# Neighbour maps turned by transposing transfers, the inverse deviation by logarithm and exponential, and a new order on every engine

## What is computed

```python
def L0(x):                       # a routed low-rank update
    w = softmax(x @ router_W.T + router_b)             # 8 experts
    y = einsum('bsr,nhr->bsnh', (x @ lora_A.T summed over 4), lora_B)   # lora_A is the context
    return nan_to_num(x + 0.5 * einsum('bsn,bsnh->bsh', w, y))
def L1(x):                       # cross attention on the context, 32 heads of 16, masked
    x = x + softmax(Q @ K.T / 4, masked) @ V @ Wo.T + bo
    mu = mean(x); var = mean((x - mu)**2)
    return (x - mu) / sqrt(var + 1e-5) * ln_g + ln_b
def L2(xyz, points, w_center, w_neighbor):   # run twice (L2, L3), the same weights
    d2 = squared distances between the 512 columns of xyz (the context)
    idx = top_k(-d2, 8)                       # 8 nearest columns of each
    for i in range(4):
        p = leaky_relu(points)
        c  = w_center[i] @ p
        gn = w_neighbor[i] @ gather(p, idx)   # for each of the 8 neighbours
        points = (c + gn.sum(over the 8)) / 9 + points
```

## Time and profile before

| what | value |
|---|---|
| median of 3 runs | 374.36 us (373.85 to 374.52) |
| the profiled execution's own time | 374.17 us |
| its span, first to last instruction | 372.4 us |
| PE busy | 365.6 us, 98% |
| PEld busy | 309.1 us, 83% |
| DVE busy | 217.8 us, 58% |
| ACT busy | 205.0 us, 55% |
| POOL busy | 123.8 us, 33% |
| DMA queues, share of 16 engines | 21.8% |

### The profile page before, as it was taken

How to read it: one execution, slowest core, us unless ns; L and a number is a source line. 1 busy time by engine, 2 the same in 40 slices (tenths; PEclk the granted TensorE clock), 3 DMA queues, 4 the chain that set the end, 5 groups by cost and what they waited for, 6 DMA issues and landing times.

```text
span 372.4 us, 6622 instructions
## 1 busy us (share of the span) xinstructions
PE 365.6 (98%) x2396; PEld 309.1 (83%) x2396; DVE 217.8 (58%) x363; ACT 205.0 (55%) x368; POOL 123.8 (33%) x125
## 2 busy tenths in 40 slices
PE   7999999999999999999999999999999999999996
PEld 4576898969878869787879899988988988989985
DVE  3946889897898867535667263343344434344334
ACT  2185357867569885475573665442843728166221
POOL 5068011430200724041072533441561445234500
PEclk9999999999999999999999999999999999999999
DMA  6993038107248117000000000000000000000004
GB/s 196 314 383 126 3 100 203 31 2 183 67 122 176 37 34 179 9 2 1 2 1 2 0 2 0 2 0 1 2 0 2 0 2 1 2 0 3 28 30 169
DMA packets 25057, 22.48 MB, mean 60 GB/s; under 512 B 9537, under 2 KB 20546, under 8 KB 25026
## 3 DMA queue, kind: packets, MB, share of 16 engines
q1 hardware_dynamic: 24352, 22.04, 21.1%
q10 hardware_dynamic: 674, 0.02, 0.1%
HBM read 12.35 MB, written 3.15 MB: 42 GB/s over the span
## 4 chain that ended last, share of the span: by engine, by line
PE 93%; SPq 3%; DMA 2%; issue 1%; DVE 0%; ACT 0%
PE slot L563 90%; SPq L495 2%; DMA xyz_n<-in_ctx 1%; DMA q_stack<-shiftT 1%; PE slot L683 1%; PE slot L724 1%; PE slot L692 1%; SPq L524 1%; PE slot L668 0%; DVE points L1333 0%; SPq L546 0%; PE slot L741 0%; SPq L447 0%; ACT low L881 0%; SPq L397 0%
## 5 line engine op out<-in xcount | busy, mean ns | idle before, releaser
L1080 POOL TENSOR_TENSOR p_lo<-p_full,p_hi 128x512 fp32r<-128x512 f32 x64 | 82.7, 1309 | 165.7 <-ACT p_full L1031 99.1
L1333 DVE SCALAR_TENSOR_TENSOR points<-slot,points 128x512 f32<-128x512 f32 x64 | 43.3, 689 | 65.6 <-PE slot L563 65.6
L1041 ACT ACTIVATE u_hi<-slot 128x512 fp32r<-128x512 f32 x64 | 36.9, 597 | 78.8 <-PE slot L563 78.7
L1328 DVE TENSOR_TENSOR u_lo<-slot,u_hi 128x512 fp32r<-128x512 f32 x64 | 42.9, 687 | 41.8 <-ACT u_hi L1041 41.7
L563 PE MATMUL slot<-adj,u_hi 128*128 128x512 f32 x256 | 66.0, 393 | 0.0
L563 PE MATMUL slot<-adj,u_lo 128*128 128x512 f32 x256 | 65.8, 391 | 0.0
L563 PE MATMUL slot<-fs_lo,p_hi 128*128 128x256 f32 x256 | 64.0, 283 | 0.0
L563 PE MATMUL slot<-fs_hi,p_hi 128*128 128x256 f32 x256 | 63.9, 283 | 0.0
L563 PEld LDWEIGHTS slot<-adj,u_lo 128*128 128x128 f32 x256 | 46.8, 188 | 9.1 <-DVE u_lo L1328 0.2
L563 PEld LDWEIGHTS slot<-adj,u_hi 128*128 128x128 f32 x256 | 46.0, 188 | 8.5
L563 PEld LDWEIGHTS slot<-fs_lo,p_hi 128*128 128x128 f32 x256 | 48.9, 191 | 0.6
(11 more groups left out here) (144 smaller groups left out, 552.4 us busy)
## 6 DMA issues: line engine op xcount, KB each, us to landing
q_stack<-q_hi SPq DMA_DIRECT2D x32, 128.0 KB, 2.4
x_in<-in_xT SPq DMA_DIRECT2D x8, 256.0 KB, 5.3
q_stack<-q_lo SPq DMA_DIRECT2D x16, 128.0 KB, 3.2
out_points<-points SPq DMA_DIRECT2D x8, 256.0 KB, 2.0
loraB_raw<-in_lora_BT SPq DMA_DIRECT2D x1, 1024.0 KB, 7.8
wk<-in_WkT SPq DMA_DIRECT2D x1, 1024.0 KB, 10.8
wq_raw<-in_WqT SPq DMA_DIRECT2D x1, 1024.0 KB, 10.5
wv<-in_WvT SPq DMA_DIRECT2D x1, 1024.0 KB, 11.4
```

The source lines that it names most:

```text
L1041: act.activation(half_of(u_hi[:, u], i % 2), bank("wa", b, i // 2, i % 2), ACT.Copy)\
L1080: pool.tensor_tensor(lo[:, cut], full[:, cut], hi[:, cut].bitcast(F32), ALU.subtract)\
L1328: dve.tensor_tensor(half_of(u_lo[:, u], i % 2), bank("wa", b, i // 2, i % 2), half_of(u_hi[:, u], i % 2).bitcast(F32), ALU.subtract).then_ ...
L1333: dve.scalar_tensor_tensor(pts, bank("ga", b, i // 2, i % 2), 1.0 / (TOPK + 1), pts, ALU.mult, ALU.add).then_inc(points_ready, 1)
```

## The change

1. The step `adjT` goes, on TensorE, with its two banks and the identity `ident_h` that POOL made for it. In its place SP issues, for each `near` step, one transposing transfer (`nt`) of a 128x512 piece of 2-byte values from SBUF to SBUF: 16 transfers of 128 KB. `adjC` now reads SBUF. The turned maps lie where other things lie at other times: that of entry 0 in `points[:, 0]`, of entry 1 in `points[:, 2]`, those of entries 2 and 3 in `near_late`, over the memory of the attention's stacks. So new waits come with it: `nt` of entry 1 waits for `vr` (a bias row lay there), `nt` of entries 2 and 3 wait for the last `w` of entry 3, `xb0` waits for `adjC0` and `xb2` for `adjC1`, and `near` of the next entry waits until the last entry's transfers have landed, since `near_of` is one buffer.
2. `dev` is a logarithm followed by an exponential with scale -0.5, which gives the reciprocal of the deviation, and the reciprocal in `ln` goes. One set of ScalarE tables is loaded ahead of everything.
3. All five tables of steps are new, with new banks; the order of every engine moves.

```diff
-                elif kind == "adjT":
-                    pe.wait_ge(idents, 2)
-                    for n in range(KC):
-                        after(pe, near_ready, "near", b, n)
...
-                    last.then_inc(turned_done, 1)
+                elif kind == "nt":
+
+                    if b == 1:
+                        sp.wait_ge(v_ready, 1)
+                    if b >= 2:
+                        after(sp, weights_done, "w", B - 1, KC - 1)
+                    after(sp, near_ready, "near", b, i)
+                    sp.dma_start_transpose(nearT[b][:, :, i * P:(i + 1) * P], near_of[:, i]).then_inc(turned_done, 16)
...
-                    after(act, turned_done, "adjT", b)
+                    act.wait_ge(turned_done, 16 * KC * (b + 1))
...
-                        after(dve, turned_done, "adjT", b - 1)
+                        dve.wait_ge(turned_done, 16 * KC * b)
...
+            act.preload_act_table_set("natural_log_exp_and_others")
...
-                    act.activation(dev[:, b], mean_var[:, b, :, 1], ACT.Sqrt, bias=eps[:]).then_inc(dev_ready, 1)
+                    act.activation(dev[:, b], mean_var[:, b, :, 1], ACT.Ln, bias=eps[:]).then_inc(act_step, 1)
+                    after(act, act_step, "dev", b)
+                    act.activation(rstd[:, b], dev[:, b], ACT.Exp, scale=-0.5).then_inc(rstd_ready, 1)
...
-                    after(dve, dev_ready, "dev", b)
-                    link(dve.reciprocal(rstd[:, b], dev[:, b]))
+                    after(dve, rstd_ready, "dev", b)
...
-kst ld_xyz2 ld_x2 ks0 qsh0 ld_x3 qs0 sd0 qsh1 ld_xyz3 qs1 ks1 sd1 ld_fs qsh2 qs2 ks2 sd2 ks3 qsh3 qs3 sd3
+nt0_3 nt0_2 nt0_1 nt0_0 nt1_0 nt1_2 ld_x2 nt1_1 nt1_3 ld_xyz2 qsh0 kst ld_x3 ks0 qs0 sd0 qsh1 ks1 qs1 ld_xyz3 sd1
+ld_fs qsh2 qs2 ks2 sd2 qsh3 ks3 qs3 sd3 nt2_2 nt2_1 nt2_3 nt2_0 nt3_2 nt3_0 nt3_3 nt3_1
```

More of the change, by code:

```diff
@@ L39 @@
 WARM_UP = 5
-POOL_LN = ()
 LOADS = "xyz0 ctxT x0 loraB wk xyz1 x1 small wq wv wo"
 PE_STEPS = """
[L48 to L51, removed]
@@ L57 @@
[L57 to L61, removed]
@@ L72 @@
-wa1_7:4,7,1 wa0_7:1,3,0 gd2_7 wb0_7 wc0_7 wb3_7 wc3_7 wd3_7 wd0_7 wb1_7 ga3_7:2,5 gb3_7 ga0_7:6,0 gb0_7 gc0_7 gc3_7
-gd3_7 wc1_7 wd1_7 gd0_7 ga1_7:2,6 gb1_7 gc1_7 gd1_7
+mb0:4 dist0_2:0 dist0_0:3 lora0:7 router0:2 dist0_1:4 dist0_3:6 mixed0:2,5 lora1:7 dist1_0:0 dist1_1:7 dist1_2:5
+ua0:6,1 ub0 uc0 values:2,3 router1:6 keys:4,5 mixed1:3,1 qa0:6,0 qb0 ua1:3,2 dist1_3:7 ub1 qc0 uc1 sc0_0:4,5 lora2:3
+sc0_1:0,1 sc0_2:2,3 router2:7 dist2_1:6 qa1:5,4 sc0_3:2,3 dist2_0:0 qb1 mixed2:7,1 lora3:2 shift0:3 qc1 router3:6
@@ new lines @@
+gd0_0 rows2:5,1 wc1_0 sc3_3:2,3 wd1_0 oa2 wa0_1:2,0,1 ga1_0:6,3 shift3:4 ob2 oc2 wb0_1 wc0_1 wd0_1 gb1_0 gc1_0
+w3_0:4,5 gd1_0 ga0_1:7,6 gb0_1 w3_1:0,1 gc0_1 gd0_1 w3_2:4,5 at3_0:0,1,2 at3_1 w3_3:6,7 wa1_1:3,5,1 at3_2 at3_3
+wb1_1 wc1_1 dist3_0:4 wd1_1 norm3:0,1 ga1_1:7,6 gb1_1 dist3_1:2 wa0_2:4,3,0 wb0_2 wc0_2 wd0_2 gc1_1 gd1_1 ga0_2:5,2
+dist3_2:1 gb0_2 rows3:0,7 oa3 ob3 oc3 wa2_0:6,1,1 gc0_2 gd0_2 wb2_0 dist3_3:7 wc2_0 wa1_2:0,3,0 wd2_0 wb1_2 wc1_2
+ga2_0:2,5 gb2_0 gc2_0 wd1_2 gd2_0 wa3_0:4,6,0 wb3_0 ga1_2:5,3 gb1_2 wc3_0 wd3_0 gc1_2 gd1_2 wa0_3:1,2,1 wb0_3
@@ L93 @@
+ph1_15 lk2_15:3 ph2_15 uh0_14 uh0_15 ph3_14 lk3_14:1 uh1_14 ph3_15 uh1_15 ph2_14 lk3_15:2 uh3_14 uh3_15 uh2_15
+uh2_14
 """
 DVE_STEPS = """
-mr init fa near0_1 a_ready fm near0_0 near0_3 near0_2 rA0 rB0 kl ml0_0 near1_1 ml0_1 rA1 vr rB1 raw0_0 nan0_0 ml1_0
-raw0_1 xl0_0 nan0_1 near1_2 ml1_1 xl0_1 mk near1_0 near1_3 raw1_0 mx0_0 nan1_0 raw1_1 mx0_1 xl1_0 nan1_1 rA2 mx0_2
-xl1_1 mx0_3 rB2 near2_0 ml2_0 sl0 ml2_1 near2_2 near2_1 raw2_0 mx1_1 mx1_0 near2_3 raw2_1 nan2_0 mx1_2 xl2_0 nan2_1
-mx1_3 xl2_1 rc0 dv0_0 dv0_1 al0_0 al0_1 rA3 sl1 rB3 mx2_0 ml3_0 st0_0 st0_1 ml3_1 ce0_1 mx2_1 ce0_0 raw3_0 nan3_0
@@ L153, in xattn_graph_kernel @@
         for part, k in enumerate(where):
-            holder[k] = (kind, b, i, 0 if kind in ("keys", "values", "adjT", "sc", "w") else part)
+            holder[k] = (kind, b, i, 0 if kind in ("keys", "values", "sc", "w") else part)
     for kind, b, i, where in act_steps:
@@ L610, in wait_read @@
                 elif kind == "rows":
[L611 to L614 removed]
+                    after(pe, centered, "ce", b, part)
                 elif kind == "wa":
```

161 lines of the change are left out of this document (65 added, 96 removed).

## The result

The changed kernel takes a median of 376.95 us (376.23 to 381.59, 17 runs) against 374.59 (373.58 to 376.19, 17 runs): ratio 1.0082, 95% interval 1.0056 to 1.0108. It is slower by 0.8%, where the forecast was 0.2% faster; the time still lies in the predicted range of 371.8 to 378.7 us.

The account below looks back on a forecast made before the run. TensorE, holding 93% of the last-ending chain, was taken to bound the kernel. Its end moves by -2.2 + 0.8 + 0.3 + 0.45 + 0.3 - 0.5 + 0.2 = -0.65 from 374.17: 373.5, rounded up to 373.6 us; range 371.8 to 378.7.

Parts of the forecast that it names:

- The start: TensorE up to the first ua product: ua0 starts at 22.1 us, which would end TensorE 2.2 us earlier.
- The transposing transfers: On SP's queue: 1.4 us to issue and 2.9 to land each; price 0.2 to 1.7 us, taken 0.8.
- the prediction's own signs of being wrong: For the transposing transfers: issues over 2 us or landings over 4 us would show the forecast wrong.
- The rival that SP is held: Transposing transfers delay near3_0 and qsh0, at 2.6 us per issue and 4 to land: 379.2 us, chance 0.22.
- w0_0: First attention w step on TensorE: TensorE ready at 75.9 us, plus 0.8 of waiting; forecast start 76.7.
- Late in entry 3: From entry 3's last w to near3_0: three issues and a landing, 7.1 us against 7.0 and 0.7 slack, cost nothing.
- ScalarE: Three table loads of 1283 ns go, 3.8 us, off the chain: 0 of it reaches the end.
- The rival of the late blocks: Entries 2 and 3 start blocks 10 to 13 us earlier, POOL's low parts could come late: 375.5 us, chance 0.09.
- TensorE's work behind the cut: TensorE from the first ua product to its end: 335.6 us before, with steps added and removed, becomes 345.0 us.
- Time outside the span: Around the profiled execution's span: 1.8 us, as in the kernel before.
- The rival of the slow pace: 1.4 us idle ahead of mixed0 brings TensorE's half pace back once, costing 2.9 us: 376.5 us, chance 0.05.

Follow-up runs that it names:

- e5: Changed kernel with one unused 32-byte tensor ahead of mask_col_i, where to_norm stood: 374.67 us, ratio 1.0008.
- e16: Changed kernel with the 32 bytes ahead of mask_col_i and five warm-up matmuls at the start, SyncE's order as changed: 374.47 us, ratio 1.0008.
- e17: Changed kernel with one unused 64-byte tensor ahead of mask_col_i: 376.58 us, ratio 1.0043.
- e9: Changed kernel with the 32 bytes ahead of mask_col_i and SyncE's order changed, kst right behind ld_x2: 374.27 us, ratio 1.0005.
- e10: Changed kernel with the 32 bytes ahead of mask_col_i, kst early and five warm-up matmuls at the start: 373.21 us, ratio 0.9969.
- e11: As e10, but with the 32 bytes right ahead of u_hi and of x1: 373.34 us, ratio 0.9977.
- e15: The kernel of e10 run again: 373.81 us, ratio 0.9996.
- e13: As e12, with six warm-up matmuls behind router0: 379.37 us, ratio 1.0096.
- e3: Kernel before with only the inverse deviation by Ln and Exp and one table set loaded at the start: 374.35 us, ratio 0.9998.
- e1: Changed kernel with two unused tensors of the old sizes where ident_h and to_norm stood: 374.83 us, ratio 1.0004.
- e6: Changed kernel with only ident_h's 256 bytes put back as an unused tensor: 378.2 us, ratio 1.0099.
- e7: Kernel before with one unused 32-byte tensor ahead of mask_col_i: 375.76 us, ratio 1.0026.
- e8: Changed kernel with 32 unused bytes right ahead of u_hi and of x1, so u is back on its place: 375.65 us, ratio 1.0031.
- e12: Changed kernel's operations in the orders of the kernel before, with the 32 bytes put back: 375.74 us, ratio 1.0033.
- e18: As e13, with adjC0 moved behind rE1 in ScalarE's order: 373.86 us, ratio 0.9979.

## Why the prediction was wrong

The sum missed by 376.95 - 373.6 = 3.35 us. By its own steps:

- **The start: right, 0.9 us too careful.** `ua0` at 21.22, not 22.1; 0.7 of it is the first distance, which starts at 5.59 instead of 6.27. Of the 0.9 us 0.3 are left at w0_0, since TensorE then waits for SyncE's queue. With `kst` late `ua0` starts at 20.7 to 21.6 in the traces of e5, e16 and e17, w0_0 at 76.7 to 77.1 all the same, with idle time before it; with `kst` early (e9, e10, e11, e15) w0_0 has none and starts 53.8 to 54.5 us after `ua0`, at 74.6 to 75.9.
- **The transposing transfers: right where they are alone, wrong under the loads of the start.** Taken were 1.4 us to issue and 2.9 to land; alone they take 1.2 and some 2.4. At the start the third and fourth took 2.6 and 2.75 us to issue, and the four landed 4.8 to 9.1 us after their issue, past both of the prediction's own signs of being wrong (issues over 2, landings over 4). It cost the changed kernel next to nothing, as TensorE's wait ahead of the keys behind it is 0.21 us; in the old orders (e13) the same landing held ScalarE for 6.7. The Trainium skill (VectorE: DVE Perf Modes, The three transpose paths) has 1309 ns for one 128x128 block; four blocks landed here 2.4 us after their issue began where nothing ran beside them, under half of the 5.2 that this rule gave as an estimate. The rival that SP is held, as it was meant for entry 3 and for `qsh0`, fell with it. (The prediction says that its range holds nearly all of that rival; the rival's own time, 379.2 us, lies above the range's end of 378.7.)
- **w0_0: right as a number**, 76.44 for 76.7, but by other waits: none for `q_stack`, where the prediction had 0.8, and 1.15 us for x_in at `lora3`, where it had 0.45 for a bank. With `kst` early (e9) neither wait is there.
- **Late in entry 3 and ScalarE: right**, nothing each (the row of `gc1_1`, and e3). The rival of the late blocks fell too, as TensorE never waits behind 107 us.
- **TensorE's work behind the cut: this is the step that failed.** The 345.0 us were 335.6 us of before's trace with steps added and taken away, as if a product cost the same in any program, and a change of place had no term at all. From w0_0 to the end the prediction has 368.6 - 76.7 = 291.9 us, measured were 294.8. The trace of e5, with 32 bytes back, has 293.0. So 1.8 us are the place of u_hi and u_lo, shown by e1, e5, e6, e17, e7 and e8; 512 matmuls at 3.4 ns each are 1.7. The diff's line `- to_norm = sb(...)` I had read as a tensor less, at no cost.
- The other **1.1 us** of that stretch are in e5 too, and only in part placed. Summed from start to start, `wa` has 31.06 us in e5 against 30.57 before, and the 20 score products behind w0_0 (`k_blk_hi,q_hi`) 5.73 against 5.22, some 0.2 of it idle. In e12 and e18, with the old orders and u on its place, both stand as before (30.57 and 5.22 to 5.23), so these 1.0 us go with the new orders. `ga` to `gd` are not among them (118.2 against 118.4), and of `wc`'s 8.09 against 7.80 the orders are not the cause, as e12 and e18 have 8.07. Which neighbourhoods of steps make it I did not take apart.
- **Time outside the span**, 2.55 us for 1.8, is the last 0.75. It isn't explained. All executions of kernels with transposes on TensorE have 1.7 to 1.9; of those with transposing transfers some have 1.8 to 1.9 throughout (e5, e10, e15), others up to 3.5 (median 2.55 after, 2.59 in e18), with no rule that I found. In the traced execution of e18 it eats most of the gain: its span is 371.5 us, 0.9 under that of the kernel before.
- **The rival of the slow pace** (0.05) was given too little. The traced execution of the changed kernel escaped it, 3 of 17 did not (clock 0.995, near 380.8 us), and e12 and e13 show its mechanism: idle time, then half clock. Filling e12's idle stretch kept it at 1.00 in e13, and with the later idle time gone as well none of e18's 11 executions stood at 0.995. In the changed kernel itself that it is the idle ahead of `mixed0` is argued, not shown: none of those three was traced. (The clock record of the trace begins at 12.2 us in the kernel before and at 9.0 in the changed one, so the 1.00 printed ahead of that says nothing of the first distances, which took 853 ns from start to start against some 455 later.)

-0.3 at w0_0, +2.9 behind it, +0.75 outside the span make the 3.35.
